# A decoder layer on one core: the transposed band masks of cross attention go from TensorE to GpSimd, in new instruction orders

## The chip, the cores and the metric

One core of one Trainium2 chip runs the whole program in one launch. The metric is the device time of one execution in microseconds (us); less is better.

## The reference, cut to what matters

32 samples (128 tokens x 128 features, float32) go through one decoder layer. After each block x is added and a layer norm without weights follows:

- **Self attention**, 16 heads of width 8, where queries, keys and values are all x itself: softmax(y y' / sqrt(8)) times x, per head, then one product with a 2048x128 matrix.
- **Cross attention**, 16 heads of width 8, queries from x, keys and values from a context of 128 tokens, with a band mask:

```python
mask = abs(i - j) <= 64                     # i: query, j: key, both 0..127
scores = where(mask, Q @ K.T / sqrt(8), -inf)
attn = softmax(scores); out = (attn @ V) @ Wo.T + bo
```

- **A local transformer of two layers** (8 heads of width 64, rotary position factors, a causal mask of 64 back, then a gated MLP), called local 0 and local 1.

## The kernel before, in words

A sample is the unit of work: all 128 tokens lie on the 128 partitions. There are four attention stages (self, cross, local 0, local 1) and two MLPs, and they work on different samples at the same time: while self attention has sample n, cross attention has n-1, local 0 has n-3 (its MLP's second part n-4), local 1 has n-4 (n-5). The dictionary `SKEW` (line 51) says this. A hardware loop of 26 passes is the main part; six iterations' worth of code ahead of it (`FILL`) fill this pipeline and a last part drains it.

Each engine has an instruction queue of its own and runs it strictly in order. What stands in it is written out by hand as strings of letters (`ORDER_TENSOR`, `ORDER_VECTOR`, `ORDER_SCALAR`, `ORDER_GPSIMD`, lines 74 to 97): one for the fill, one for the loop's pass, one for the drain. A letter stands for the next step of a stage: S self, Z self's values (x times the 2048x128 matrix), C cross, A and B the first parts of local 0 and 1, D and E their score parts, M and N the MLPs' first, O and P their second parts; W is a filler product. A stage is a Python generator, each `yield` ends a step, and `weave` (line 154) takes the steps in the string's order; a letter whose stage has no step left does nothing. Between engines only semaphores order the work (`wait_ge`, `then_inc`).

The attention core of self and cross (`core16`, line 626) on TensorE goes like this, by two pairs of head groups (a group is four heads and one PSUM bank of 512 columns):

- `head_scores` (593): natural scores, query on the partition, in bf16. For cross, `mask_band` (573) adds a mask of 0 or -1e30 by products of a mask tile with the identity: four products of 64x64 by 256 columns for a pair. VectorE takes the row maxima with negative sign (`head_max`, 1032).
- A transpose turns the negative maxima; ScalarE copies them back (`shifts`, 872).
- `turned_scores` (607): the transposed scores, key on the partition, in float32 (L611), then the maxima added by small products (L617), and for cross again `mask_band` (L579). ScalarE makes the exponentials into `s.e` in SBUF (`exps`, 877), four instructions of 128x512.
- Cross then sums with the tile `own` for the denominators (L717) and with V for the numerators (L724). Both wait for all exponentials. VectorE takes the reciprocal (L1108), multiplies (L1112), and TensorE projects (L729).

Each pair of cross has its own wait: the second pair's transposed scores wait for the first pair's exponentials, since they use the same two banks. The banks of self and cross are also lent to the MLPs of local 0 and 1.

GpSimd has no access to PSUM and does small SBUF work: products with the reciprocal denominators of the local layers (L1313), rotary additions (L1296, L1300), inverse roots by a power (L1245, L1292), copies and bias additions.

Of the kernel before, what the change touches and what calls it, by code (L numbers as in the profile page):

```python
# [34 lines left out]
GH = 4  # L35
# [39 lines left out]
    ("SZSZSZSSSZSSSSSSSSWWWWWWWWWWWSCCZSZCCSZCCSZCSCSCCSCSCCSSCSSCSCLSAASCAACSZZZSCCAZSASSCCDDCSSCCCSSCCCSSDCDSCDCSD"  # L75
     "MAAMAOOCAOCSBZBSCZBSCABSASSZZDCSSCDBBSCSCCCEECCCSSDDSCDCSDCEMEEMAOEONAAONSBPPBAPBZZSCBCSAZASZSSCCDDBBCSSCEECSS"
     "CCCDSSDCCDCSDSCEEMCECME"),
    ("ONAOAONABPSPBABPZSCZBSACAZSDSCSDCZSSCCBBSSCEECCCSDDSSDCCCSDEEMCCECME"),
    ("ONAOAONASPBPABSBPZZSCBACSZSSCCAZSCSCDDBCBSSCCEECSDCCCDSSCCDECSEDEMAEAMNOOAAONBPPBBPAACBCDCDCBBCCECECCCDCCCDCCD"
     "CEDEMAEAMEOOAAOBNBAABDDBWWWWWWWBNBDEEDPDDEMEPMEOOEPOBNBWWWNBPBPWWWWWWBBWWEEWWWWWWWWWWWWPEEWWEWWENWWWWWWWNPPWWP"))  # L80
ORDER_VECTOR = (
    ("SSSSSSSSSSSSSSSSSSSCCCSSCCSSCCLSSSSCSSSCSSCCSCLSSSSSAAAAACSCSCASSCCCCDDDSDSSDSDSSSCSCSSCSCSDMCMMSMSASAOAOCCCAA"
     "SSBBSSBBBCACCCDSDDSBSDODEESDSSSEESSECSCSESDCMMMSCMSCENNNONAOAAPABBABSPSSBBSSCCCABCCDDDPCCDEEDESOSDSSESSSEESSSD"
     "MSSCPMMCSMCCSECS"),
    ("NNNONOAAAAPABBPSSBPSSCCCABBDCDCBCDCSDSDESEDSESSESSPSESESSDSMSMMCCSMCOCEC"),
    ("NNNONOAAAAPASBBSPBSSBCCCBACCPCCDDDBSDDSESEDEESSSESOSCECSSSCCSDMCMMSMENSNNAAONAOPAAASOPBBPBBBCCCPBCCDDCCDDDEEED"
     "EECCPECCDCMMMMEAAAOAAOANBNBBBDNDBDBNDDDEEEEEDEMMMOMPOEOPNPNNNBBBBBBEEEEEPPEPENOPNNPNPPPP"))
# [6 lines left out]
ORDER_GPSIMD = (
    ("SSSSCSCSSASACAAAABDDCAMMSSASOAAABBBABBDDECEMMCNSNBASASAAABBBBABDODCEPEMMCS"),
    ("ONBSANASABAAPBABBBDDEECSMMC"),
    ("NSNOSBACAAAABBBBPABDDEECMMNNBSAAAAABBBBABCDDEPECMMNBOAAAAAABBNBBDBDEMEMNNBBBOOBBBPEENPNP"))
ORDER_SYNC = (
# [1268 lines left out]
```

## Time and profile before

| | |
|---|---|
| median of 3 runs | 1370.85 us (1366.49 to 1371.11) |
| the profiled execution | 1365.17 us, span 1363.4 us |
| TensorE busy | 1298.9 us, 95% |
| VectorE busy | 1069.0 us, 78% |
| ScalarE busy | 979.1 us, 72% |
| GpSimd busy | 761.7 us, 56% |
| one pass of the loop | 39.93 us |
| granted clock of TensorE | 0.991 of full |

Busy times count what an engine executes, not waits. The ends of matrix products are modelled, so two products that overlap show more time than they hold the queue: the distance between two starts is the price. Since the loop repeats exactly, an instruction seen at 602.02 us is also found at 641.95, one period later. "Released by" behind an idle time names what the engine waited for.

### The profile page before, as it was taken

How to read it: one execution, taken by the hardware profiler on the slowest of the kernel's cores; microseconds unless marked ns; L12 is line 12 of the kernel's file. 1: busy time of each engine (PE TensorE's matmuls, PEld its weight loads, DVE VectorE, ACT ScalarE, POOL GpSimd, SP SyncE). 2: the span in 40 equal slices, each digit the busy share in tenths (PEclk: the TensorE clock that was granted, in tenths of full speed). 3: DMA queues.
4: the chain of work that ended last, by engine and by line, in shares of the span. 5: the costliest groups of instructions: out<-in, count | busy, mean ns of one | idle time of the engine just before them, and what ended most of it. 6: DMA issues, size and time to landing. Idle time of an engine off the chain costs nothing. (4 is left out here: it accounts for less than half of the span.)

```text
span 1363.4 us, 41792 instructions
## 1 busy us (share of the span) xinstructions
PE 1298.9 (95%) x13550; PEld 906.1 (66%) x13550; DVE 1069.0 (78%) x3190; ACT 979.1 (72%) x2688; POOL 761.7 (56%) x843
## 2 busy tenths in 40 slices
PE   5999999999999999999999999999999999999876
PEld 2566666777766677766667777666777666776653
DVE  3667888888888888888888888888888888888743
ACT  2357777777787777778777777777777777777753
POOL 1135666555666555566655566565556666555653
PEclk9799999999999999999999999999999999999989
DMA  5000000000000000000000000000000000000000
GB/s 168 11 5 2 6 8 7 6 2 6 6 6 4 6 6 2 6 6 6 4 6 6 2 6 6 4 6 6 6 2 6 6 4 6 6 3 4 6 1 6
DMA packets 21042, 12.44 MB, mean 9 GB/s; under 512 B 4700, under 2 KB 19846, under 8 KB 20998
## 3 DMA queue, kind: packets, MB, share of 16 engines
q1 hardware_dynamic: 18790, 8.04, 2.2%
q10 hardware_dynamic: 2208, 3.84, 0.8%
q8 instruction: 24, 0.39, 0.1%
q14 instruction: 20, 0.16, 0.0%
HBM read 9.78 MB, written 2.10 MB: 9 GB/s over the span
## 5 line engine op out<-in xcount | busy, mean ns | idle before, releaser
L1292 POOL TENSOR_TENSOR local_rn<-local_sc,half_neg 128x8 f32<-128x8 f32 x128 | 211.0, 1649 | 69.3 <-DVE local_sc L1143 69.3
L1313 POOL TENSOR_TENSOR local_e<-local_e,local_rd 128x512 f32<-128x512 f32 x128 | 133.3, 1041 | 197.2 <-DVE local_rd L1160 197.2
L954 ACT ACTIVATE local_e<-local_ps,local_bias,local_rn 128x128 f32<-128x128 f32 x512 | 229.4, 468 | 13.2 <-DVE local_bias L1156 13.1
L668 PE MATMUL self_ps<-self_z,self_e 128*128 128x129 f32 x1024 | 146.0, 285 | 2.4 <-ACT self_e L881 1.1
L690 PE MATMUL local_ps<-wz,self_kT 128*128 128x512 f32 x256 | 138.2, 625 | 5.9 <-ACT self_kT L887 5.7
L1075 DVE SCALAR_TENSOR_TENSOR self_y<-self_ps,self_rd,self_y 128x128 f32<-128x128 f32 x448 | 133.1, 345 | 9.5
L668 PEld LDWEIGHTS self_ps<-self_z,self_e 128*128 128x128 f32 x1024 | 127.4, 192 | 11.6 <-DVE self_y L1075 2.3
L1296 POOL TENSOR_TENSOR local_cosp<-local_cosp,local_sinp 128x512 f32<-128x512 f32 x64 | 81.4, 1272 | 87.1 <-DVE local_sinp L1135 87.0
L1151 DVE TENSOR_REDUCE local_m<-local_ps 128x4 f32<-128x512 f32 x128 | 87.9, 687 | 39.0 <-PE local_ps L589 38.2
L934 ACT ACTIVATE local_sq<-local_ps 128x512 f32<-128x512 f32 x128 | 76.0, 594 | 48.4 <-PE local_ps L750 43.6
L954 ACT ACTIVATION_READ_ACCUMULATOR local_e<-local_ps,local_bias,local_rn 128x1 f32 x512 | 109.8, 215 | 0.0
L1036 DVE TENSOR_REDUCE self_neg<-self_ps 128x4 bf16<-128x512 f32 x128 | 82.6, 686 | 27.5 <-PE self_ps L598 26.7
L881 ACT ACTIVATE self_e<-self_ps 128x512 f32<-128x512 f32 x128 | 69.7, 596 | 34.7 <-PE self_ps L617 34.6
L1131 DVE TENSOR_TENSOR local_cosp<-local_ps,cos_t 128x512 f32<-128x512 f32 x128 | 87.8, 686 | 7.1 <-ACT local_sq L934 6.3
L1036 DVE TENSOR_REDUCE cross_neg<-cross_ps 128x4 bf16<-128x512 f32 x128 | 86.5, 683 | 6.9 <-PE cross_ps L579 6.6
L961 ACT ACTIVATE local_eT<-local_ps 128x512 f32<-128x512 f32 x128 | 70.6, 597 | 27.8 <-PE local_ps L789 27.7
L965 ACT ACTIVATE local_oT<-local_ps 128x512 f32<-128x512 f32 x64 | 39.5, 617 | 68.7 <-PE local_ps L797 68.7
L904 ACT ACTIVATE self_z<-local_ps 128x512 f32<-128x512 f32 x128 | 76.0, 599 | 16.6 <-PE local_ps L690 14.7
L1135 DVE TENSOR_TENSOR local_sinp<-local_ps,sin_t 128x512 f32<-128x512 f32 x128 | 87.0, 680 | 0.0
L1140 DVE TENSOR_REDUCE local_ss<-local_sq 128x8 f32<-128x512 f32 x128 | 86.3, 674 | 0.0
L1300 POOL TENSOR_TENSOR local_cosp<-local_cosp,local_sinp 128x512 f32<-128x512 f32 x64 | 81.1, 1267 | 1.5 <-DVE local_sinp L1135 1.4
L750 PE MATMUL local_ps<-wqkv_s,local_xT 128*128 128x512 f32 x128 | 70.3, 632 | 6.6 <-ACT local_xT L930 6.6
(179 smaller groups left out, 3322.8 us busy)
## 6 DMA issues: line engine op xcount, KB each, us to landing
self_xin<-x SPq DMA_DIRECT2D x32, 64.0 KB, 1.8
cross_cin<-ctx_in SPq DMA_DIRECT2D x32, 64.0 KB, 1.8
out<-local_out SPq DMA_DIRECT2D x32, 64.0 KB, 1.6
wqkv_s<-wqkv ACTq DMA_DIRECT2D x2, 768.0 KB, 9.7
wz<-w_heads ACTq DMA_DIRECT2D x4, 256.0 KB, 5.9
w_r<-w ACTq DMA_DIRECT2D x2, 341.0 KB, 11.0
con<-consts SPq DMA_DIRECT2D x1, 640.0 KB, 6.7
wo_s<-wo ACTq DMA_DIRECT2D x2, 256.0 KB, 10.8
```

The costliest lines, as they stand in the source:

```text
L668: last = nc.tensor.matmul(bank[:, 129 * j:129 * j + 129], s.e[:, h0 + j, :], s.z[:, h0 + j, :], start=True, stop=True)
L690: nc.tensor.matmul(LOC[l].b1 if g % 2 else LOC[l].b0, s.kT[:, :], wz[:, 512 * g:512 * g + 512], start=True, stop=True).then_inc(s.z_psum, 4)
L954: nc.scalar.activation(s.e[:, a, p, :], bank[:, 128 * p:128 * p + 128], ACT.Exp, bias=s.bias[:, a, p:p + 1], scale=s.rq[:, a, p:p + 1], ac ...
L1036: nc.vector.tensor_reduce(s.neg[:, 32 * g:32 * g + GH], (s.odd if g % 2 else s.even).rearrange("p (j t) -> p j t", j=GH), AX.X, ALU.max, n ...
L1075: nc.vector.scalar_tensor_tensor(out=s.y[:, h % 2, :], in0=bank[:, j, 0:128], scalar=s.rd[:, h:h + 1], in1=before, op0=ALU.mult, op1=ALU.a ...
L1131: nc.vector.tensor_tensor(s.cosp[:, a, :, :], heads, cos_t[l][:, a, :].unsqueeze(1).to_broadcast([128, LH, LD]), ALU.mult)\
L1135: nc.vector.tensor_tensor(s.sinp[:, a, :, :].rearrange("p h (u d) -> p h u d", u=2), halves[:, :, ::-1, :], sin_t[l][:, a, :].rearrange("p ...
L1140: nc.vector.tensor_reduce(s.ss[:, LH * a:LH * a + LH, 0:1], s.sq[:, a, :, :], AX.X, ALU.add)\
L1151: nc.vector.tensor_reduce(s.m[:, a, :], bank.rearrange("p (c t) -> p c t", c=LH // 2), AX.X, ALU.max, negate=True)\
L1292: nc.gpsimd.tensor_tensor(s.rn[:, heads], s.sc[:, heads], half_neg[:, 0:LH], ALU.pow).then_inc(done, STEP)
L1296: nc.gpsimd.tensor_tensor(s.cosp[:, 0, :, :], s.cosp[:, 0, :, :], s.sinp[:, 0, :, :], ALU.add).then_inc(s.k_roped, STEP)
L1313: nc.gpsimd.tensor_tensor(s.e[:, a, :, :], s.e[:, a, :, :], s.rd[:, a, :].unsqueeze(2).to_broadcast([128, LH // 2, 128]), ALU.mult)\
```

## The change

`mask_band` is no longer called for the transposed scores (it still is for the natural ones). The exponentials outside the band are therefore some finite number, and GpSimd sets them to zero in `s.e`: two `affine_select` instructions for each pair of head groups, each over 8 heads and one half of the query columns, 128x512 elements in all. Denominators and numerators wait for a new semaphore `band_done` in place of `exp_done`. Cross attention has two steps fewer on TensorE and two more on GpSimd. The order strings of all engines are new. In the loop's string of GpSimd most letters do nothing, since their stage has no step left.

```diff
...
 ORDER_TENSOR = (
...
-    ("ONAOAONABPSPBABPZSCZBSACAZSDSCSDCZSSCCBBSSCEECCCSDDSSDCCCSDEEMCCECME"),
+    ("ONAOAONABPSPBAPBSCBZSZCZSAASCSCDDZCSSCBBSSEECSDCCSDCCDSDSEEMCCECME"),
...
 ORDER_VECTOR = (
...
-    ("NNNONOAAAAPABBPSSBPSSCCCABBDCDCBCDCSDSDESEDSESSESSPSESESSDSMSMMCCSMCOCEC"),
+    ("NNNONOAAAPABBPSSAASSBCCCBBCCDDDBCCPDSSDSEESDSSEESESESOSDSSSMMSMCCMCCPECS"),
...
 ORDER_SCALAR = (
...
-    ("KOAANBAPSBASYBZCZBAASCZSSZDSSBBDCDDEEDDCCEEDCCEEEM"),
+    ("KOAANBPSABASBCBYZZCSAAZSSZDSSBBDDDCEECCDDEEDCCEEEM"),
...
 ORDER_GPSIMD = (
...
-    ("ONBSANASABAAPBABBBDDEECSMMC"),
+    ("NSNNNNNNBNNNAASOAAAAOBAAAAABOAAAAABBBBBBBOBBBBBAAAAAODAAABBBBBBDDEDAACBBCEBEBBDDDDCPPPPPEEBEBAAMEDEBMBDSSSSMSS"
+     "SSESESSSSMMMMAMMMACCCCCCCCCCCCCCCCC"),
...
 ORDER_SYNC = (
-    "CSP")
+    "SPC")
...
@@ -309,6 +310,7 @@
         CROSS.o_ready = sem("cross_o_ready")
         CROSS.proj_psum = sem("cross_proj_psum")
         CROSS.x_bias = sem("cross_x_bias")
+        CROSS.band_done = sem("cross_band_done")
         LOC[0].kept = sem("local0_kept")
         LOC[1].base_bias = sem("local1_base_bias")
         for s, n in ((SELF, "self"), (CROSS, "cross")):
@@ -615,13 +617,10 @@
                     for g in pair:
                         rows = slice(32 * g, 32 * g + 32)
                         last = nc.tensor.matmul(scores_bank(s, g)[:, 128 * j:128 * j + 128], hot_b[rows, j, :], s.negT[rows, :],
-                                                start=False, stop=(j == GH - 1 and not s.windowed), skip_group_check=True)
-                        if j == GH - 1 and not s.windowed:
+                                                start=False, stop=(j == GH - 1), skip_group_check=True)
+                        if j == GH - 1:
                             last.then_inc(s.scores_t_psum, 4)
                 yield
-                if s.windowed:
-                    mask_band(s, pair, s.scores_t_psum)
-                    yield
 
             def core16(s, v):
 
@@ -711,7 +710,7 @@
                 yield
                 yield from core16(s, v)
 
-                pe.wait_ge(s.exp_done, v + STEP)
+                pe.wait_ge(s.band_done, v + STEP)
                 for j in range(GH):
                     for g in range(G):
                         last = nc.tensor.matmul(s.b1[32 * g:32 * g + 32, 0:128], own[:, j, 32 * g:32 * g + 32],
@@ -1269,6 +1268,16 @@
                     pool.wait_ge(s.resid, v)
                 nc.gpsimd.tensor_tensor(s.xb[:, :], s.x[:, :], bo_r[:, :], ALU.add).then_inc(s.x_bias, STEP)
                 yield
+                for k, pair in enumerate(s.pairs):
+                    pool.wait_ge(s.exp_done, v + 8 * k + 8)
+                    heads = slice(GH * pair[0], GH * pair[0] + 2 * GH)
+                    late = s.e[:, heads, 64:128]
+                    nc.gpsimd.affine_select(late, late, [[0, 2 * GH], [-1, 64]], ALU.is_ge, 0.0, base=0, channel_multiplier=1)\
+                        .then_inc(s.band_done, 4)
+                    early = s.e[:, heads, 0:64]
+                    nc.gpsimd.affine_select(early, early, [[0, 2 * GH], [1, 64]], ALU.is_ge, 0.0, base=64, channel_multiplier=-1)\
+                        .then_inc(s.band_done, 4)
+                    yield
                 inverse_root(s, v, s.moments, s.ve, s.rs[:, :], s.rstd)
                 yield
```

In words, as far as the loop's pass is concerned, TensorE's steps from local 0's K product to cross attention's denominators are, before and after (`ts` transposed scores, `hs` natural scores, `m` the masks behind them, 0 and 1 the pair, `av` self attention's products with the values in sets of three heads):

```
before: ... self negT, D scores, self ts0, cross hs0, D mask, cross hs0 m, Z, self ts1, cross hs1, m, B qT, kT,
        self av0, av1, cross negT, E scores, E mask, cross ts0, m, self av2, D eT0, eT1, self av3, av4, D av,
        cross ts1, m, self av5, D projection, E eT0, eT1, M shift, cross denominators
after:  ... self negT, A qT, kT, self ts0, cross hs0, m, D scores, D mask, Z, cross hs1, self ts1, cross m, B qT, kT,
        self av0, av1, E scores, E mask, cross negT, self av2, D eT0, cross ts0, self av3, D eT1, cross ts1, D av,
        self av4, D projection, self av5, E eT0, eT1, M shift, cross denominators
```

ScalarE's from self attention's third group of exponentials on (`e` exponentials):

```
before: self e2, e3, B qT, kT, D e, cross negT, D e (two steps), E e (two), D eT0, eT1, cross e0, e1, E e (two), D oT, cross e2, e3
after:  self e2, e3, B qT, kT, D e (three steps), cross negT, E e (two), cross e0, e1, D eT0, eT1, E e (two), D oT, cross e2, e3
```

GpSimd's from local 0's weights on:

```
before: D weights 0, 1, E weights 0, 1, cross x + bias, S root, M bias, M root, C root
after:  D weights 0, 1, E weights 0, cross x + bias, selects of pair 0, E weights 1, selects of pair 1, P root, M bias, M root, S root, C root
```

## Rows read from the trace of the kernel before

**Rows 1.** The page, part 1: busy us (share of the span) and instructions, whole run.
```profile
PE 1298.9 (95%) x13550; PEld 906.1 (66%) x13550; DVE 1069.0 (78%) x3190; ACT 979.1 (72%) x2688; POOL 761.7 (56%) x843
```

**Rows 2.** Busy time by window, one period: length, then busy us (x instructions) per engine.
```profile
600.81:640.74 39.93, 39.33 (x425) 27.90 (x421) 33.20 (x99) 30.48 (x85) 23.70 (x27) 1.00 0.02 5
```

**Rows 3.** Busy time by window: ahead of the loop, the loop, behind it.
```profile
0.00:188.00 188.00, 164.72 (x1517) 104.71 (x1518) 123.58 (x374) 103.05 (x269) 74.61 (x93) 0.95 0.12 35
188.00:1227.00 1039.00, 1023.27 (x10955) 725.55 (x10954) 864.00 (x2578) 792.79 (x2185) 616.67 (x678) 1.00 0.02 5
1227.00:1364.00 137.00, 110.95 (x1080) 75.83 (x1078) 81.42 (x242) 83.23 (x236) 70.39 (x74) 0.97 0.02 4
```

**Rows 4.** Timeline of TensorE, 600 to 645 us: start us, duration us, instruction, count.
```profile
600.47 0.41 PE L589 MATMUL local_ps<-mask_n,ident_b 64*64 64x512 bf16 x4
...
607.75 0.30 PE L579 MATMUL cross_ps<-mask_w,ident_b 64*64 64x256 bf16 x4
607.99 0.49 PE L668 MATMUL self_ps<-self_z,self_e 128*128 128x129 f32 x2
...
610.34 1.08 PE L717 MATMUL cross_ps<-cross_e,con 128*32 128x128 f32 x32
...
617.48 1.10 PE L750 MATMUL local_ps<-wqkv_s,local_xT 128*128 128x512 f32 x2 [0.15 <-ACT local_xT L930]
...
636.31 0.40 PE L598 MATMUL cross_ps<-cross_kb,cross_qmb 32*128 32x128 bf16 x8
636.63 0.30 PE L579 MATMUL cross_ps<-mask_w,ident_b 64*64 64x256 bf16 x4
636.87 0.66 PE L763 MATMUL local_ps<-con,local_cosp 128*128 128x128 f32 x4
```

**Rows 5.** Timeline of ScalarE, 600 to 641 us.
```profile
601.37 0.22 ACT L954 ACTIVATION_READ_ACCUMULATOR local_e<-local_ps,local_bias,local_rn 128x1 f32 x1
602.02 0.46 ACT L954 ACTIVATE local_e<-local_ps,local_bias,local_rn 128x128 f32<-128x128 f32 x1 [0.44 <-DVE local_bias L1156]
...
607.46 0.64 ACT L965 ACTIVATE local_oT<-local_ps 128x512 f32<-128x512 f32 x1
608.15 1.08 ACT L881 ACTIVATE cross_e<-cross_ps 128x512 f32<-128x512 f32 x2
...
636.63 1.08 ACT L881 ACTIVATE self_e<-self_ps 128x512 f32<-128x512 f32 x2
```

**Rows 6.** Groups by line and form: busy us, mean ns, idle before.
```profile
L881 ACT ACTIVATE cross_e<-cross_ps 128x512 f32<-128x512 f32 x128 | 69.8, 603 | 1.7 <-PE cross_ps L579 0.4
...
L579 PE MATMUL cross_ps<-mask_w,ident_b 64*64 64x256 bf16 x512 | 38.2, 289 | 0.0
```

**Rows 7.** Timeline of VectorE, 600 to 641 us.
```profile
600.99 0.69 DVE L1151 TENSOR_REDUCE local_m<-local_ps 128x4 f32<-128x512 f32 x1 [0.82 <-PE local_ps L589]
...
601.77 0.16 DVE L1156 TENSOR_TENSOR local_bias<-local_m,local_rn 128x4 f32<-128x4 f32 x1
```

**Rows 8.** Groups by line and form, GpSimd: busy us, mean ns, idle before.
```profile
L1313 POOL TENSOR_TENSOR local_e<-local_e,local_rd 128x512 f32<-128x512 f32 x128 | 133.3, 1041 | 197.2 <-DVE local_rd L1160 197.2
L1296 POOL TENSOR_TENSOR local_cosp<-local_cosp,local_sinp 128x512 f32<-128x512 f32 x64 | 81.4, 1272 | 87.1 <-DVE local_sinp L1135 87.0
...
L1226 POOL TENSOR_SCALAR mask_n<-con 128x512 bf16<-128x512 f32 x2 | 1.2, 620 | 4.4 <-DMA bo_r<-bo 4.4
L1226 POOL TENSOR_SCALAR mask_w<-con 128x256 bf16<-128x256 f32 x2 | 0.8, 407 | 0.0
...
L1226 POOL TENSOR_SCALAR ident_b<-con 128x128 bf16<-128x128 f32 x1 | 0.3, 301 | 0.7 <-DMA con<-consts 0.7
```

**Rows 9.** Timeline of TensorE, the last sample's cross denominators.
```profile
1281.62 1.08 PE L717 MATMUL cross_ps<-cross_e,con 128*32 128x128 f32 x32 [0.64 <-ACT cross_e L881]
```

More of the change, by code:

```diff
@@ L88 @@
-ORDER_SCALAR = (
-    ("SSSZSSZZZSSSCSCSZZCSSCCZZSSCCAASACSAZCZSZAASSCZDSSCCDDDCCDDDKAMAAOCACSBSZBZBYSABSASZZSSBBCDDCCDDECCEDDEEDEEMEA"
-     "OANABPBASSZBCZBCAZSZASSBBDSDSCDDECCEDDEEDCCEEEM"),
-    ("KOAANBAPSBASYBZCZBAASCZSSZDSSBBDCDDEEDDCCEEDCCEEEM"),
-    ("KOAANSABPSABYBZZCBSCZASSASZSBCDBDDDCCEDECCEDEDEEEAKMAOAANBPBYBCAABCBBDDCDDCCDECCEDEEDEEAEMAKOAABBAABBDDDBDBNDD"
-     "EEDEEPEEMEOBBNBBBBPYEEEEKEEENP"))
+    ("SZSZSZSSSZSSSSSSSSCWWWWWWWWWWWSCZSCCZCCSZZCSCSCSCSCSSSCCSSCLSSAAASCACSZZSZCCSAAZCSCSDDCSSCCSSCCSSDSCSDCDCDMAAM"
+     "COOACOBSABZZSBCBSCAZASZSSCDCSSDCBBSCCEESCCSDSDSCCDCSDEMEEMAOEONAAOSBANBPPZBSBPZSCZACSAZSCSCDDBBSCSCEESCSCCDSCC"
+     "DSSDSCCDEEMCEME"),
@@ new lines @@
+    ("ONAOAONABPSPBAPBSCBZSZCZSAASCSCDDZCSSCBBSSEECSDCCSDCCDSDSEEMCCECME"),
+    ("ONOAOABSABBNAPPSZBZPSACAZCSZSSCCDDSSCBBCSEECSCCSSDCCSDSEDCCECDEMAEANMAOONAOPBPBBPAACBCDDCCBCCBCDCCEECCDDCCECDE"
+     "MAEAMEAOONOBABAABDDBWWWWWWWBBNEEDDDPDMEEPMEOOEPOBNBBWWWNBPPWWWWWWBWWWWWWWWWWWWPBWWEEEEWWEWWENWWWWWWWNPPWWP"))
+ORDER_VECTOR = (
+    ("SSSSSSSSSSSSSSSSSSSCCCSCCSCSCSLSSSSCCSSCSCSLCSSSSSSASAAAACSSCCSSCCCCADDSDSSDDSSSSDSSSCSSCSCCSDCMMMMSAAOCOCAACA"
+     "BBBOSSBBSSCCABCCDDSDSDDEESSDESSSESSCCSECSECSDMMMCMSENNSONAOANASAABBPBSBSPSBSCCCAOCCDBDDDCCSPDESEDSSSSESESSESSE"
+     "SSCDCMSMMCMPCSCE"),
+    ("NNNONOAAAPABBPSSAASSBCCCBBCCDDDBCCPDSSDSEESDSSEESESESOSDSSSMMSMCCMCCPECS"),
+    ("NNONONAAAABBASPBSBPSBSPCCCACCDDBDCCSDSEDSESESSDSEESESCCSCCSDSMCMMSEMNOSNNAANOAOAPAAPSBBPBBBCCCDDCCDDDCCBDPEEEE"
+     "ECCECCDMOCMMMEAAAOAAONANNOBBBBDDBBNDDDDEPEEEEDEMMMMPOENPONPNNBBBPBBBPEEPOEEPEEENPNNNPPPP"))
@@ L94 @@
+ORDER_SCALAR = (
+    ("SSSZZZSSZSSCSSCZZCSZCCSSZCCSSAASACSAZZCASZASSCZSSCCDDCCDDDDDKAMAOCCABSABSBZZBYASZAZSSSSBCBDDCCDDCCDEEDEEDEEMEA"
+     "OASBANABPSZBBZCZSACAZSSBBDSSDCDDCCDECCDEEEDEEEM"),
+    ("KOAANBPSABASBCBYZZCSAAZSSZDSSBBDDDCEECCDDEEDCCEEEM"),
+    ("KOABASANBSBAPZBZYCZCSAAZSSSBBSDDCDECCDEDCCDEEDEKEEAAMONABPABBACACYBDDBDBCDDCCCCDEEDEEKEEAEAMAOBABAABBDDBBDDDED"
+     "NEDEEPEEMEOBBNBBPYBBEEEEEEEKNP"))
 ORDER_GPSIMD = (
-    ("SSSSCSCSSASACAAAABDDCAMMSSASOAAABBBABBDDECEMMCNSNBASASAAABBBBABDODCEPEMMCS"),
@@ L96 @@
[L96 to L97 removed]
+    ("SSSSSCCCCSSSAOAAAABACCDCDCMSSMAASAAABBCBABBDCDCEEMCMNSSBNAOAASBABABBACBDDPCCEEMMSC"),
+    ("NSNNNNNNBNNNAASOAAAAOBAAAAABOAAAAABBBBBBBOBBBBBAAAAAODAAABBBBBBDDEDAACBBCEBEBBDDDDCPPPPPEEBEBAAMEDEBMBDSSSSMSS"
+     "SSESESSSSMMMMAMMMACCCCCCCCCCCCCCCCC"),
+    ("NSONBASAABAABCBBABDCDECECOPMMNBSNAAAAAACBBBBDBOODCCEECMMPNBAAAAANABBBBBDDEMEMNNBPBBBBBEEPNNP"))
 ORDER_SYNC = (
[L99 removed]
+    "SPC")
```

10 lines of the change are left out of this document (removed).

## The prediction

> **What bounds the kernel now.** I read the page's busy times first: TensorE is busy 95% of the span, ScalarE 72%, GpSimd 56% [rows 1]. Then one pass of the loop: a period lasts 39.93 us and repeats to the hundredth, with TensorE busy for 39.33 of it, ScalarE for 30.48 and GpSimd for 23.70 [rows 2]. The 26 passes make 1039 of the 1363 us; ahead of them lie 188 us and behind them 137 us, in which TensorE is less full (165 and 111 us busy) [rows 3]. So in the loop TensorE's own queue sets the time, and time taken off that queue comes back in full, unless another engine makes TensorE wait. The timelines of one period show how near that is. From the first K product of local layer 0 (617.48) to the end of self attention's last transposed scores (636.31) TensorE never waits: 18.83 us. From there to cross attention's denominators (610.34, one period on 650.27) it takes 13.96 us, also without a wait [rows 4]; but ScalarE ends the last cross exponentials at 608.15 + 1.08 = 609.23 [rows 5], only 1.11 us before the denominators start. From the denominators to the next 617.48 are 7.14 us, with short waits: a chain over reciprocal, output projection, norm and transpose. That stretch keeps its instructions and, on TensorE, its order. So the period is 18.83 + 13.96 + 7.14 = 39.93, and the change has to be placed in it.
>
> **Removed.** Per sample TensorE loses eight mask products on the transposed scores: two groups of four. A group holds the queue from 607.75 to 607.99, or 0.24 us [rows 4] (the products, 289 ns each, overlap [rows 6]). That is 0.48 us per sample, 12.5 us in 26 passes and 15.4 us in all 32 samples. This is the most that the change can give from that part, some 1.1%.
>
> **Moved, first stretch.** Cross attention's second pair of natural scores (636.31 to 636.63, 0.32 us [rows 4]) now goes before self attention's last transposed scores. The first stretch becomes 18.83 + 0.32 = 19.15 us, the second loses the same 0.32. Following the new lists of the other engines I find no new wait in the first stretch: what they have to deliver (rotated Q and K, copies to SBUF, maxima) is there some tenths before it is used.
>
> **Moved, second stretch.** TensorE's own work there is now 13.96 - 0.32 - 0.48 = 13.16 us. ScalarE does the same list of work in it, in another order. I count from the end of self attention's last transposed scores. Local layer 1's mask group, at 640.40 (600.47 one period on) or 4.09 before, comes at 4.09 - 0.32 = 3.77. From that group to the first of this layer's exponentials pass 602.02 - 600.47 = 1.55 us, by way of the maximum and the bias on VectorE [rows 4, 5, 7]; I take 1.5, as a reciprocal no longer stands between the two. So these exponentials start at 5.27. ScalarE could take them at 4.9 (its list from 636.63 to 601.59 + 39.93 = 641.52 lasts 4.9 at most, and now begins some 0.15 after the scores), so it waits as before. From these exponentials to the end of the last cross exponentials ScalarE is packed: 609.23 - 602.02 = 7.21 us [rows 5]. The same work in the new order ends at 5.27 + 7.21 = 12.48. Ahead of the last two exponentials stands the copy of local layer 0's attention output, ending at 12.48 - 1.08 = 11.40; only with it can TensorE go on to that layer's output projection. From there self attention's last product, projection, transposes and shift take what 607.99 to 610.34 shows, 2.35 us [rows 4] (before, the short product stood first and the copy was there in time; now it stands behind the projection). So TensorE comes to the denominators at 13.8, not at 13.16: of the 0.48 us saved and the earlier score pair, 0.64 is lost again to ScalarE's queue.
>
> **Added: the selects.** GpSimd gets four affine selects per sample, each over 8 heads x 64 columns, 128x512 f32 in place. Their throughput is no matter: GpSimd has 39.93 - 23.70 = 16.2 us free per period [rows 2], so four may cost 4 us each before it becomes the bound. Their latency counts: the first pair's selects lie behind other work, but the denominators wait for both selects of the last pair. The trace has no select, so I bound it. Nearest below is a one-input operation of the same size, 620 ns; the 301 and 407 ns of the same operation with 128 and 256 elements show that this is a fixed 0.2 us and 0.83 ns per element. Above stand two-input operations of 1041 and 1272 ns [rows 8]. A select reads one input but also has to form and compare an index; I take 0.75 us, near the one-input row, and keep 0.6 and 1.27 for the range. Nothing excludes more. The Trainium skill (GPSIMD Engine Reference, Performance pitfalls for Q7 kernels) says that compare-then-select bodies run at 2.03 cycles per element as written and 1.03 when unrolled twice; an estimate from that page's 1.2 GHz and the fixed 0.2 us would be 1.07 or 0.64 us, that is, either end of my bounds, and no row here tells which.
>
> The denominators can then start at 12.48 + 0.1 (a hand-over between engines, as 601.68 to 601.77 on [rows 7]) + 2 x 0.75 + 0.05 = 14.1, against 13.8 by TensorE's own queue. **Period:** 19.15 + 14.1 + 7.14 = 40.4 us, 0.46 more than now, and 12 us in 26 passes. With 0.6 us per select it is 40.1 (+0.15, 4 us in all), with 1.04 it is 41.0 (+1.05, 27 us), with 1.27 41.4 to 41.6 (+40 us). Behind the last pair's selects on GpSimd stand three inverse roots and a bias addition; the nearest needed one, for layer 0's second norm, is wanted only after the reciprocal of the denominators (0.96 us), by which time it is ready, so I cost that at nothing. If that cover were gone it would be some 0.5 us per pass. GpSimd's selects of the first pair take the place ahead of layer 1's second weights; with 0.75 they end before those can start, so again nothing; from 1 us up they push the last pair's by some 0.2.
>
> **Outside the loop** six samples lose 0.48 us each (2.9 us) where TensorE is full, and where it is not, the wait for the last exponentials (0.64 us before the last denominators, [rows 9]) grows by two selects and a hand-over, 1.65 us, in perhaps two or three samples. I set the two against each other: zero, within 4 us. No DMA is added or moved past anything that waits: SyncE's list has its three independent steps in another order, and they are prefetches by most of a period.
>
> **Sum.** The profiled execution took 1365.2 us for a span of 1363.4; with +12 it would be 1377. The median of the three runs is 1370.85, 5.7 above the profiled one; a forecast for the median lies between 1377 and 1383, and I say 1381.
>
> **The rivals.** (a) *No change* (27%): the selects cost about 0.6 us, and the period comes out within 0.25 us of 39.93: 1364 to 1377. Measurement of this kernel can tell about 0.5%, 7 us, from no change. For it: the one-input row. Against: the select's extra work. (b) *Faster* (28%): the removed 0.48 us counts in full, 26 x 0.48 + 2.9 = 15 us, so 1356, or half of that. The place is the copy of layer 0's attention output on ScalarE: if that stands ready when TensorE has finished its product (10.8 by TensorE's own starts, against the 11.4 of my chain), and a select stays under (13.16 - 12.0 - 0.15) / 2 = 0.5 us with ScalarE that much earlier, TensorE remains the only bound. Against it is the packed ScalarE stretch; for it is that my 0.64 is a difference of long sums, good to 0.3. (c) *Clearly dearer selects* (14%): 1.04 us and more, as two-input rows; 1371 + 27 = 1398 or more; the denominators become the longest wait in the loop. In its extreme GpSimd is the bound from 4 us per select. The Trainium skill (GPSIMD Engine Reference, Elementwise side-by-side cycle accounting) gives about 12 cycles per element for data-dependent branching; by that page an estimate is 5.1 us per select, and the change would be a disaster; I give that 2 of the 14. (d) That the change does not take the masks out can be left aside: the diff leaves the natural scores' masks alone and removes the call for the transposed ones.
>
> **How the numbers follow.** My forecast (selects of 0.68 to 0.95 us, +8 to +22 us) has 31%. With (c) slower by over 0.5% has 45%, within 0.5% 27%, faster 28%. The range has to reach into (b), to 1359, and up to the two-input price, 1401; about 8% lies below and 10% above. The forecast's own range is 1376 to 1393.
>
> **What would show it.** Of the changed kernel I expect: no mask products after the transposed scores (256 in place of 512); a select at 0.75 us; a period of 40.4; denominators that start 0.15 us after a select's end, with TensorE idle there for 0.3 us in every period, named as waiting for GpSimd; and a wait of TensorE before layer 0's output projection, named as ScalarE's copy. If the period is 39.5 with no such waits, the ScalarE chain is what I got wrong; if the wait is there but longer, it is the select's price.

## The result and the profile after

The changed kernel takes 1392.98 us (median of 4 runs, 1388.37 to 1394.04), the one before 1369.2 in the same session: a ratio of 1.0185, 95% interval 1.0162 to 1.0207, so slower, by 1.6 to 2.1%. The profiled execution took 1392.2 us for a span of 1390.3, 26.9 more than the 1363.4 of before. The forecast was 1381 with 1359 to 1401 as the range: the sign and the range held, the size did not. The median is 24 us above that of before, where the forecast's sum had +12 and its 1381 was 10 above the median it started from.

The page, part 1, of the changed kernel (against [rows 1]):

```profile
PE 1315.7 (95%) x13289; PEld 902.7 (65%) x13294; DVE 1072.7 (77%) x3190; ACT 976.1 (70%) x2688; POOL 841.7 (61%) x971
```

TensorE has 261 instructions fewer (of the 256 mask products and a few missing records) and is nevertheless busy for 17 us more: its products took longer somewhere. GpSimd has its 128 selects, 84 us by their groups (shown at the end).

Where the time went is read from one instruction per sample, the transpose of self attention's input. Timelines of TensorE, the seventh and the last of the 32, first after, then before:

```profile
230.30 0.27 PE L653 MATMUL self_ps<-con,self_x 128*128 128x128 f32 x1
...
1233.93 0.27 PE L653 MATMUL self_ps<-con,self_x 128*128 128x128 f32 x1
```

```profile
221.45 0.27 PE L654 MATMUL self_ps<-con,self_x 128*128 128x128 f32 x1
...
1218.95 0.27 PE L654 MATMUL self_ps<-con,self_x 128*128 128x128 f32 x1
```

The time up to the seventh (I call it the fill) is 8.85 us longer, the 25 periods between the two take 1003.6 in place of 997.5 (some 0.25 each), and from the last to the end, the drain, it is 1390.3 - 1233.93 = 156.4 in place of 1363.4 - 1218.95 = 144.45. So of 26.9 us the loop's passes have 6 to 7 and **the two ends have 20.8**. Some 4.7 of the 8.85 in the fill are no property of the kernel: they belong to a slow start that some executions of either kernel show (under e7).

The loop first. Busy time by window of the changed kernel, one period (against [rows 2]), then TensorE's and GpSimd's timelines around the denominators of that period (against [rows 4]):

```profile
588.77:628.97 40.20, 39.59 (x413) 27.48 (x414) 33.30 (x100) 30.37 (x84) 26.22 (x30) 1.00 0.02 5
```

```profile
607.83 0.30 PE L581 MATMUL cross_ps<-mask_w,ident_b 64*64 64x256 bf16 x4
...
611.52 0.41 PE L591 MATMUL local_ps<-mask_n,ident_b 64*64 64x512 bf16 x4
...
619.18 1.16 PE L802 MATMUL local_ps<-wo_s,local_oT 128*128 128x128 f32 x8
620.18 0.39 PE L667 MATMUL self_ps<-self_z,self_e 128*128 128x129 f32 x2
620.40 1.04 PE L788 MATMUL local_ps<-con,local_e 128*128 128x128 f32 x8
621.46 0.41 PE L816 MATMUL self_ps<-local_mid,con 128*128 128x64 f32 x2
621.80 1.08 PE L716 MATMUL cross_ps<-cross_e,con 128*32 128x128 f32 x32
...
628.97 0.67 PE L749 MATMUL local_ps<-wqkv_s,local_xT 128*128 128x512 f32 x1 [0.15 <-ACT local_xT L929]
```

```profile
620.24 0.66 POOL L1275 TENSOR_SCALAR_AFFINE_SELECT cross_e<-cross_e 128x512 f32<-128x512 f32 x1
620.85 0.66 POOL L1278 TENSOR_SCALAR_AFFINE_SELECT cross_e<-cross_e 128x512 f32<-128x512 f32 x1
```

The three stretches are 607.83 - 588.77 = 19.06, 621.80 - 607.83 = 13.97 and 628.97 - 621.80 = 7.17. The selects start 0.61 us apart and end at 621.51, 0.29 before the denominators, which follow the shift's product with no wait.

Now the ends. TensorE in the fill, after and then before:

```profile
32.88 0.46 PE L667 MATMUL self_ps<-self_z,self_e 128*128 128x129 f32 x2 [0.34 <-DVE self_y L1074]
36.83 0.45 PE L703 MATMUL cross_ps<-con,cross_cin 128*128 128x128 f32 x1 [3.48 <-DVE cross_x L1051]
...
37.71 3.29 PE L854 MATMUL local_ps<-hot_b,ident_b 128*128 128x512 bf16 x10 [0.22 <-issue]
40.83 0.27 PE L653 MATMUL self_ps<-con,self_x 128*128 128x128 f32 x1
```

```profile
28.77 2.54 PE L855 MATMUL local_ps<-hot_b,ident_b 128*128 128x512 bf16 x11
32.38 0.30 PE L654 MATMUL self_ps<-con,self_x 128*128 128x128 f32 x1 [1.08 <-issue]
32.62 0.30 PE L704 MATMUL cross_ps<-con,cross_cin 128*128 128x128 f32 x1
```

The fillers (products on a constant, which only keep TensorE busy) stood between attention and the next norm's result, where TensorE had nothing to do. The new order puts cross attention's transposes, which need that result, ahead of them: TensorE waits 3.48 us and then works off the fillers with everything ready. In the drain the changed TensorE waits for VectorE's row maxima and then runs slowly; the last sample's cross scores, after:

```profile
1287.50 0.40 PE L600 MATMUL cross_ps<-cross_kb,cross_qmb 32*128 32x128 bf16 x8 [0.60 <-DVE cross_qm L1100]
...
1290.26 0.39 PE L600 MATMUL cross_ps<-cross_kb,cross_qmb 32*128 32x128 bf16 x8 [1.55 <-DVE cross_neg L1035]
...
1292.60 0.26 PE L638 MATMUL cross_ps<-ident_b,cross_neg 128*128 128x128 bf16 x1 [1.13 <-DVE cross_neg L1035]
...
1293.65 2.08 PE L613 MATMUL cross_ps<-cross_qm,cross_kT 32*128 32x512 f32 x4
```

Before, the same four score products took 1.13 us behind shorter waits (0.68, 0.48 and 0.45 us). The windows name the cause: the granted clock (the third column from the end) is 0.62 and 0.70 after, and 1.00 from 1275 to 1295 in before, which holds the same work (counted from the last of the 32 transposes, both are 56 to 76 us). Busy time by window, after and then before:

```profile
1290.00:1300.00 10.00, 8.61 (x57) 5.11 (x59) 4.62 (x14) 5.55 (x19) 4.97 (x5) 0.62 0.01 2
1300.00:1310.00 10.00, 8.92 (x128) 6.89 (x124) 3.19 (x11) 7.80 (x24) 3.40 (x5) 0.70 0.00 0
...
1370.00:1380.00 10.00, 8.53 (x59) 5.54 (x60) 1.57 (x7) 3.29 (x6) 2.04 (x4) 0.62 0.01 3
```

```profile
1275.00:1285.00 10.00, 8.28 (x146) 5.67 (x147) 4.75 (x14) 9.59 (x36) 4.02 (x5) 1.00 0.01 2
```

The low stretch at 1370 has a wait in front of it as well. Twelve fillers stood behind the last score masks before; in the new order they run ahead of the scores, at 1359.03, and nothing is left to cover the softmax. TensorE before, then after:

```profile
1339.96 0.41 PE L589 MATMUL local_ps<-mask_n,ident_b 64*64 64x512 bf16 x4
1340.30 2.76 PE L855 MATMUL self_ps<-hot_b,ident_b 128*128 128x512 bf16 x12
```

```profile
1359.03 2.75 PE L854 MATMUL self_ps<-hot_b,ident_b 128*128 128x512 bf16 x12
...
1364.82 0.41 PE L591 MATMUL local_ps<-mask_n,ident_b 64*64 64x512 bf16 x4
1369.77 1.11 PE L788 MATMUL local_ps<-con,local_e 128*128 128x128 f32 x4 [4.53 <-POOL local_e L1322]
```

### The profile page after: what moved, and what is told of

Read it like the earlier page. It is cut to its first block and busy times, and to the rows that moved or that the text cites. A ratio compares the mean times of both kernels' runs of the same rounds, so it can differ in the third digit from the quotient of the medians.

```text
span 1390.3 us, 41520 instructions
## 1 busy us (share of the span) xinstructions
PE 1315.7 (95%) x13289; PEld 902.7 (65%) x13294; DVE 1072.7 (77%) x3190; ACT 976.1 (70%) x2688; POOL 841.7 (61%) x971
## 5 line engine op out<-in xcount | busy, mean ns | idle before, releaser
L667 PE MATMUL self_ps<-self_z,self_e 128*128 128x129 f32 x1024 | 151.7, 287 | 3.5 <-ACT self_e L880 2.5
L953 ACT ACTIVATION_READ_ACCUMULATOR local_e<-local_ps,local_bias,local_rn 128x1 f32 x512 | 120.8, 236 | 0.0
L903 ACT ACTIVATE self_z<-local_ps 128x512 f32<-128x512 f32 x128 | 73.1, 594 | 49.1 <-PE local_ps L689 49.1
L1244 POOL TENSOR_TENSOR local_rs<-local_ve,half_neg 128x1 f32<-128x1 f32 x96 | 55.8, 582 | 61.7 <-DVE local_ve L1180 54.7
L1035 DVE TENSOR_REDUCE cross_neg<-cross_ps 128x4 bf16<-128x512 f32 x128 | 82.3, 684 | 5.5 <-PE cross_ps L581 5.1
L788 PE MATMUL local_ps<-con,local_e 128*128 128x128 f32 x512 | 75.1, 279 | 7.4 <-POOL local_e L1322 7.3
```

The source lines that it names most:

```text
L667: last = nc.tensor.matmul(bank[:, 129 * j:129 * j + 129], s.e[:, h0 + j, :], s.z[:, h0 + j, :], start=True, stop=True)
L953: nc.scalar.activation(s.e[:, a, p, :], bank[:, 128 * p:128 * p + 128], ACT.Exp, bias=s.bias[:, a, p:p + 1], scale=s.rq[:, a, p:p + 1], ac ...
L1035: nc.vector.tensor_reduce(s.neg[:, 32 * g:32 * g + GH], (s.odd if g % 2 else s.even).rearrange("p (j t) -> p j t", j=GH), AX.X, ALU.max, n ...
```

## The experiments

An order is three strings per engine (ahead of the loop, the loop, behind it). The table has the ratio to the kernel before, and, of each profiled execution, the fill, the period and the drain as defined above; the sections below refer to it.

```
                     ratio (95%)               span    fill    period  drain
before               1                         1363.4  221.45  39.93   144.45
after                1.0185 (1.0162, 1.0207)   1390.3  230.30  40.20   156.37
e1_old_edges         1.0118 (1.0089, 1.0148)   1378.3  226.19  40.20   148.03
e2_old_orders        1.0108 (1.0079, 1.0137)   1377.2  225.50  40.08   150.66
e3_old_fill          1.0171 (1.0138, 1.0205)   1388.3  227.62  40.20   157.09
e4_old_drain         1.0111 (1.0081, 1.0142)   1386.5  231.29  40.20   151.11
e5_late_fillers      1.0167 (1.0139, 1.0194)   1386.6  225.74  40.20   157.24
e6_cross_fillers     1.0121 (1.0092, 1.0151)   1383.6  230.53  40.20   149.43
e7_fillers_first     1.0156 (1.0129, 1.0183)   1385.0  223.69  40.20   157.65
e8_no_masks          0.9988 (0.9969, 1.0007)   1365.3  225.40  39.86   144.21
e9_selects_aside     1.0184 (1.0162, 1.0206)   1385.4  225.47  40.20   156.26
e10_one_group_kept   1.0042 (1.0023, 1.006)    1367.7  222.87  39.99   145.80
e11_scores_earlier   1.0094 (1.0076, 1.0111)   1374.7  222.36  40.19   148.37
e12_both_edges       1.009  (1.0073, 1.0106)   1383.6  226.83  40.21   152.92
```

The fill of after, e4, e6, e8 and e12 contains the slow start, that of the others doesn't; only fills with the same start can be compared.

The first set splits the new orders from the selects.

**e1_old_edges.** The selects and the loop's new strings stay; the strings ahead of and behind the loop are those of before, adapted.

```diff
-TENSOR, VECTOR, SCALAR, GPSIMD = (new fill, new loop, new drain)
+TENSOR, VECTOR, SCALAR, GPSIMD = (old fill, new loop, old drain)
+# old: less TensorE's two steps C of masks, plus two steps C of selects on GpSimd
```

> The changed kernel's loop orders, but fill and drain in the orders of the kernel before (the steps of the transposed masks taken out, GpSimd's selects put in where the exponentials ended in the trace of before). Theory A (the orders of fill and drain cost 20 of the 27 us: fillers that moved onto the path in the fill, TensorE at the half clock in the drain): the period stays 40.20, the fill is within 3 us of before's, the drain within 4 us of before's, and the time is 7 to 13 us above before. Rival B (the selects' latency costs it where TensorE is not full, whatever the order): the edges stay 15 to 20 us longer than before's and the time is 22 to 27 us above before.

Measured: +1.18%, some 16 us, with 6.6 in the loop, 4.7 in the fill and 3.6 in the drain of the profiled execution. That is above the 7 to 13 us of theory A and below the 22 of rival B. The new orders at the ends cost about 0.7%, 9 us, by themselves. It doesn't come down to my loop term alone: with selects the ends stay some 8 us above before. The timeline of this kernel names most of that. At four of its denominators outside the loop TensorE waits for GpSimd's select, 6.0 us together (the fourth, at 173.68, is 0.99); before waited 0.64 at one of the four.

```profile
86.07 1.08 PE L707 MATMUL cross_ps<-cross_e,con 128*32 128x128 f32 x32 [1.91 <-POOL cross_e L1269]
...
1258.85 1.08 PE L707 MATMUL cross_ps<-cross_e,con 128*32 128x128 f32 x32 [1.56 <-POOL cross_e L1269]
...
1296.37 1.94 PE L707 MATMUL cross_ps<-cross_e,con 128*32 128x128 f32 x32 [1.57 <-POOL cross_e L1269]
```

**e2_old_orders.** The same with the loop's strings too.

```diff
-TENSOR loop "ONAOAONABPSPBAPBSCBZSZCZSAASCSCDDZCSSCBBSSEECSDCCSDCCDSDSEEMCCECME"
+TENSOR loop "ONAOAONABPSPBABPZSCZBSACAZSDSCSDCZSSCCBBSSCEECCSDDSSDCCSDEEMCCECME"
-GPSIMD loop (new)
+GPSIMD loop "ONBSANASABAAPBABBBDDCCEECSMMC"
```

> The whole change in masks and selects, but every part in the orders of before, with the same insertions. Theory A: the denominators now wait for the second select, 609.23 + 0.1 + 2 x 0.63 = 610.6 against 609.86 by TensorE's own queue, so the period is 39.93 - 0.48 + 0.74 = 40.2, the same as with the new orders, and the time is 7 to 13 us above before. Rival B: period 40.2 but 22 us or more above before. Rival C (the new orders hide the selects and the old ones do not): period 40.7 or more.

Timeline of TensorE, the denominators of one period:

```profile
615.76 1.08 PE L707 MATMUL cross_ps<-cross_e,con 128*32 128x128 f32 x32 [0.22 <-POOL cross_e L1269]
```

Here the wait for the selects does show, 0.22 us, and yet the period is 40.08, shorter than the 40.20 of the new order, which has no such wait. The reordering buys nothing in the loop. The period is 0.1 under the 40.2 of theory A, the time, 14 us above before, a little over its 13.

**e3_old_fill** and **e4_old_drain** take back one end each.

```diff
-(new fill, new loop, new drain)
+(old fill, new loop, new drain)     # e3
+(new fill, new loop, old drain)     # e4
```

> The changed kernel with only the fill in before's orders. Theory A: the loop and the drain stay as in the changed kernel (40.20; 154 us from the last self transpose to the end), the fill gets 3 to 8 us shorter: the time is 17 to 23 us above before. Rival B: no gain, 25 us above before.

> The changed kernel with only the drain in before's orders. Theory A: from the last self transpose to the end 142 to 147 us in place of 154, with at most two short stretches at the half clock in it: 13 to 18 us above before. Rival B: 154 us stays, 25 us above before. Rival D (the half clock in the drain is chance of the one execution profiled): the clock is full but the median time is no better than the changed kernel's.

The old drain gives 0.7%, 10 us of 24. The old fill gives 0.14%, inside both intervals: the expected 3 us and more didn't show. The profiles say why. e3's fill is 227.62, and with the same start the new fill takes 225.74 (e5) and 225.47 (e9): the old one has no misplaced fillers, but waits 1.91 and 1.00 us for selects, as in e1. So the 9 us of e1 are those of the drain. The drain of e4 is 151.1, 4 above the most I expected: the granted clock is low there too (0.69 from 1293 to 1303).

The second set changes single places of the ends.

**e5_late_fillers.** In the drain's tail the last scores of the local layers go ahead of the twelve fillers again.

```diff
-...WWWWWWBWWWWWWWWWWWWPBWWEEEEWWEWWENWWWWWWWNPPWWP
+...WWWWWWBBWWEEWWWWWWWWWWWWPEEWWEWWENWWWWWWWNPPWWP
```

> The changed kernel with one edit in TensorE's drain string: its last 47 letters in before's order, which puts twelve filler products behind local layer 1's last scores, where TensorE sits idle for 4.5 us, in place of ahead of them. Theory A (the drain is longer because TensorE falls to the half clock behind idle stretches): the 10.2 us at the half clock near the end shrink to 3.4 or less, and the time falls by 3 to 5 us against the changed kernel. Rival B (the drain is longer by the selects' latency, and the clock costs nothing on a chain of waits): within 1 us of the changed kernel.

A miss: -0.2% with overlapping intervals, and a drain as long as before the edit. In its profile the window from 1370 has a clock of 0.80 in place of 0.62, but from the last cross denominators to the end it takes 86.4 us, where the changed kernel takes 85.6 and before 81.8. So this place alone is not shown to be worth anything, and the 4 us of the tail are not explained.

**e6_cross_fillers.** e5, and 13 more fillers (2, 6 and 5) where TensorE waits for the row maxima of the last sample's cross scores.

```diff
-..."CDDCCBCCBCDCC"...
+..."CDDWWCCBWWWWWWCCBWWWWWCDCC"...
-wait_ge(LOC[0].resid, STEP * (B - 1 if n < EARLY_GAPS else B))
+wait_ge(LOC[0].resid, STEP * (B - 2 if n < 13 else B - 1 if n < 13 + EARLY_GAPS else B))
```

> As the run before, and thirteen more filler products, in the three waits of TensorE for row maxima among the last sample's cross scores (2, 6 and 5 of them; 0.21 us each at the full clock). Theory A: the 13.7 us at the half clock around the last cross scores go, and the time falls by another 5 to 7 us, to some 9 to 11 below the changed kernel. Rival B: no change, or 1 to 2 us more for the added products.

Confirmed: 0.64% less than the changed kernel, some 9 us (0.46% less than e5), by adding work to TensorE. Timeline of TensorE and a window of this kernel:

```profile
1291.53 1.24 PE L846 MATMUL self_ps<-hot_b,ident_b 128*128 128x512 bf16 x5
...
1293.47 1.13 PE L605 MATMUL cross_ps<-cross_qm,cross_kT 32*128 32x512 f32 x4
```

```profile
1293.00:1303.00 10.00, 8.50 (x154) 5.98 (x153) 4.21 (x12) 8.15 (x29) 6.20 (x7) 1.00 0.01 2
```

The score products start at 1293.47 against 1293.65, so the wait itself was worth 0.2 us. They take 1.13 against 2.08 us, and the last denominators come at 1300.16 in place of 1304.67: what the waits cost was the clock behind them, 4.3 of the 4.5 us up to there. The profiled executions agree. Counted from the last of the 32 transposes:

```
                                              to the last cross denominators   clock, 60 to 70 us
before; e8                                    62.7; 62.3                       1.00; 0.83
new drain (after, e3, e5, e7, e9)             70.7, 70.6, 70.9, 70.9, 70.7     0.50 in all five
new drain with the 13 fillers (e6, e12)       66.0, 66.8                       1.00, 0.83
old drain with the selects (e1, e2, e4)       66.1, 66.5, 66.5                 0.59, 0.54, 0.57
```

All five executions of the new drain without these fillers take 2.08 us for the score products, both with them 1.13: this fall of the clock is no chance. The 3.4 to 3.8 us that the old drain with selects stands above before are its waits for them (1.56 and 1.57 us in e1, against 0.64) and the slower products behind.

**e7_fillers_first.** One letter of the fill moved: cross attention's transposes behind the fillers.

```diff
-SZSZSZSSSZSSSSSSSSCWWWWWWWWWWWSC...
+SZSZSZSSSZSSSSSSSSWWWWWWWWWWWCSC...
```

> The changed kernel with one letter of TensorE's fill string moved: the first cross transposes stand behind the eleven filler products again, so that the fillers run while the first norm is computed. Theory A: the distance between the first two self transposes falls by 3 us (35.9 to 33 with the late rise of the clock, 28 to 29 without), and so does the time. Rival: later waits in the fill take it back, and the time stays within 1 us. The slow first products up to 28 us are the same instructions as in before, so I expect them to be chance: in some executions the clock rises at 15 to 18 us here too.

-0.3%, 4 us, but the intervals overlap, so the time alone doesn't show a gain; the profiles do. Self attention's second transpose comes at 33.14 in place of 40.83. Only about half of that is the order. The rest is a state of this execution, the slow start: in the profiles of the changed kernel, e4, e6, e8 and e12 the first score products of self attention take 2.08 us, in the other nine 1.13, with the same instructions up to there.

```profile
18.67 2.08 PE L613 MATMUL self_ps<-self_qm,self_kT 32*128 32x512 f32 x4 [0.43 <-ACT self_negT L874]
```

```profile
18.42 1.13 PE L604 MATMUL self_ps<-self_qm,self_kT 32*128 32x512 f32 x4 [0.43 <-ACT self_negT L865]
```

The twelfth run has the same slow start and e7's order, and from self attention's last products to its next transpose it takes 37.20 - 32.85 = 4.35 us where the changed kernel takes 40.83 - 32.88 = 7.95: the order's part is 3.6 us. With a fast start it is less: up to the seventh transpose e7 is 1.8 and 2.1 us ahead of e9 and e5, and with the slow start e12 is 3.5 ahead of the changed kernel. e9 and e5 have the changed kernel's fill and a fast start: against the 230.30 of the changed kernel that puts the slow start at 4.6 to 4.8 us, and what the fill itself costs above before at 4.0 to 4.3, not 8.85.

**e12_both_edges.** e6 and e7 in one kernel.

> The changed kernel with the three edits on TensorE's edge strings together (fillers ahead of the first cross transposes, fillers behind local layer 1's last scores, thirteen fillers in the last sample's cross waits). Theory A: the gains add, 3 to 4 us in the fill and 8 to 10 in the drain: 12 to 14 us above before, of which the loop has 7. Rival: a low clock comes back elsewhere in the drain, and it stays at 16 or more above before.

1.0090, and 1.0185 without the three edits: 13 us of 25 come back, as theory A has it, though the clock fell once more in this execution's drain (0.70 from 1360 to 1370).

The third set asks what the mask products and the selects are worth by themselves.

**e8_no_masks.** The kernel before without the masks on the transposed scores and with nothing in their place, its orders less those steps. Half of cross attention's mask is left out.

```diff
-                if s.windowed:
-                    mask_band(s, pair, s.scores_t_psum)
-                    yield
```

> The kernel before with the band masks on the transposed scores left out and nothing in their place: weights outside the band stay, so cross attention is computed without half of its mask. It measures the removal by itself, in before's orders. By the sum in the prediction the period falls by all of 0.48 us to 39.45 and the time by 12 to 15 us. Rival (ScalarE's chain is the bound there already): the period falls by 0.2 or less, the time by under 6 us.

This decides the question of the gain in the orders of before. TensorE has 0.48 us less to do per sample, and the period falls by 0.07. Even with no selects at all the removal brings 0.12% (-0.31% to +0.07%). TensorE's timeline of this kernel shows where the rest stays:

```profile
603.76 0.41 PE L581 MATMUL local_ps<-mask_n,ident_b 64*64 64x512 bf16 x4
...
611.42 1.16 PE L792 MATMUL local_ps<-wo_s,local_oT 128*128 128x128 f32 x8
612.42 1.04 PE L778 MATMUL local_ps<-con,local_e 128*128 128x128 f32 x8
613.29 0.33 PE L806 MATMUL self_ps<-local_mid,con 128*128 128x64 f32 x2
613.56 1.08 PE L706 MATMUL cross_ps<-cross_e,con 128*32 128x128 f32 x32
```

and ScalarE's:

```profile
605.31 0.46 ACT L943 ACTIVATE local_e<-local_ps,local_bias,local_rn 128x128 f32<-128x128 f32 x1 [0.44 <-DVE local_bias L1145]
...
610.71 0.66 ACT L954 ACTIVATE local_oT<-local_ps 128x512 f32<-128x512 f32 x1
```

From local layer 1's mask group to its first exponentials it is 605.31 - 603.76 = 1.55 us, as before; from there ScalarE's list reaches the copy of layer 0's output after 5.40, before 607.46 - 602.02 = 5.44 [rows 5]. The copy ends 611.37 - 603.76 = 7.61 us after the mask group here and 608.10 - 600.47 = 7.63 before, and 0.05 behind it the output projection starts. So the chain from the mask group over VectorE and ScalarE takes the same time with or without the two mask groups that TensorE does meanwhile: they lay beside it. From the copy's end to the denominators it is 2.19, and 2.24 before; with 7.61 for 7.63 that is all of the 0.07. In before the projection started only 0.21 behind the copy, so TensorE's queue could gain little there. TensorE, before:

```profile
608.31 1.06 PE L803 MATMUL local_ps<-wo_s,local_oT 128*128 128x128 f32 x8
```

**e9_selects_aside.** The changed kernel with its selects on a tile of zeros, and the denominators waiting for the exponentials alone. The same half of the mask is left out.

```diff
-                pe.wait_ge(s.band_done, v + STEP)
+                pe.wait_ge(s.exp_done, v + STEP)
-                    late = s.e[:, heads, 64:128]
+                    late = s.aside[:, heads, 64:128]
```

> The changed kernel in its own orders, with the same selects on a tile beside the exponentials (of zeros), so that GpSimd is as busy and the denominators wait for the exponentials alone; the weights outside the band stay in, so cross attention is computed without that half of its mask. Theory A (ScalarE's chain is what bounds the new loop, the selects stand a hair behind it): the period falls from 40.20 by 0.1 us at most, to 40.1, still above before's 39.93 with 0.48 us of TensorE work gone; the time falls by 2 to 6 us against the changed kernel, edges included. Rival B (the wait for the selects is the loop's cost): the period falls by the whole of it and of the masks, to 39.7 or less.

A period of 40.20 and a ratio of 1.0184 against 1.0185: in the new orders nothing waits for the selects, in the loop or at the ends (its drain is 156.26, the changed kernel's 156.37).

The last two try for a version that beats both, on the kernel before's orders.

**e10_one_group_kept.** GpSimd's selects for three of the four groups of heads (two of 128x512, two of 128x256), TensorE's mask for the last, whose exponentials end latest.

```diff
+kept = s.pairs[1][1] if s.windowed and pair == s.pairs[1] else None
-if s.windowed: mask_band(s, pair, s.scores_t_psum)
+if kept is not None: mask_band(s, (kept,), s.scores_t_psum)
```

> A version between the two, in before's orders: GpSimd selects on three groups, and TensorE keeps its mask (two of eight products) for the last group, whose exponentials end last, so that no select stands behind the last exponentials. The denominators should wait for nothing new. By ScalarE's chain (theory A) the period is that of the run without masks, 39.86 to 39.93, and the time equal to before within 3 us. Rival C (TensorE's removed work counts as soon as no select is waited for): period 39.57, 9 to 11 us below before.

**e11_scores_earlier.** e10 with local layer 1's scores one product of self attention earlier in the loop, so that the chain of e8 starts sooner.

```diff
-TENSOR loop ...BBSSCEECSC...
+TENSOR loop ...BBSECESCSC...
-SCALAR loop ...BBDCDDEEDDCCEE...
+SCALAR loop ...BBDDCDEECCDDEE...
```

> The run before, with two edits in the loop's strings: TensorE makes local layer 1's scores and mask ahead of self attention's second value product, and ScalarE takes the first cross exponentials ahead of local 0's copies. ScalarE's 0.44 us of waiting for the bias inside its packed stretch should go. Theory A: the chain gets shorter by about 0.4 us, TensorE's removed work shows for the first time, and the period falls to 39.5 to 39.8; the time is 3 to 10 us below before. Rival C (ScalarE is not the bound): the period stays where the run before has it, or rises by the wait that the new place gives TensorE (0.3).

e10 is at +0.42%, 4 us, period 39.99: no gain, and by its interval a small loss, just outside the 3 us of theory A. e11 is at +0.94%, period 40.19, a miss: the scores now wait for their own input, and VectorE's bias is still late. TensorE and ScalarE of this kernel:

```profile
602.06 1.16 PE L776 MATMUL local_ps<-local_kT,local_qT 64*128 64x128 f32 x16 [0.22 <-ACT local_kT L940]
```

```profile
605.08 0.46 ACT L949 ACTIVATE local_e<-local_ps,local_bias,local_rn 128x128 f32<-128x128 f32 x1 [0.36 <-DVE local_bias L1151]
```

No version beat the kernel before. In before's orders e8 bounds what the removal can give, 2 us; that another order would shorten the chain and give more is not excluded, e11 only failed to.

## Why the prediction was right in sign and wrong in size

**What failed: "Outside the loop ... I set the two against each other: zero, within 4 us."** It was 20.8 us of the profiled 26.9, and still about 16 with the 4.7 of the slow start taken off: 4 in the fill, 12 in the drain. I weighed there what six samples lose in masks and gain in waits for selects, and didn't go through the new strings of the fill and the drain, which I had gone through for the loop. Three things stand in them: fillers behind a product that waits instead of ahead of it (e7, e12: 2 to 3.6 us); the last cross scores waiting 0.60, 1.55 and 1.13 us for VectorE without fillers, with half the clock behind them (e6: some 9 us, together with e5's edit, which alone showed 0.2% at most); and the fillers of the tail ahead of the scores, for which no price was shown. e1 puts the new orders of both ends at 9 us, e3 and e4 lay that in the drain, and e12 mends 13. The wait that I did weigh, two selects and a hand-over before the last denominators, isn't in the changed kernel at all (e9). It is in the old orders, at four samples and not two or three, and is most of the 8 us that remain in e1. What the tail behind the last cross denominators takes longer, some 4 us, stays open.

**The loop.** The period came near in part by luck: the path was right up to the projection of local layer 0, but behind it two terms were off in opposite directions, and the selects did not decide. First stretch 19.15 forecast, 19.06 measured; third 7.14, 7.17. In the second the mask group came 3.69 us in (3.77 forecast), and the output projection 7.66 later, at 11.35 (11.40 forecast, by ScalarE's copy): the wait that I expected is among the waits of the changed kernel's weight loads as 13.0 us in 55 times, 0.7 at the longest.

```profile
PEld local_ps L802 <- ACT local_oT L964: 13.0, 55, 0.7
```

The denominators came at 13.97: 13.8 was forecast by TensorE's queue and 14.1 by the selects. One mis-sized term is the **select: 0.75 us taken, 0.66 measured** and 0.61 from start to start. The nearest row, the one-input operation of 620 ns [rows 8], should have been taken as it was; forming and comparing an index costs nothing that shows. The last select ended at 621.51 - 607.83 = 13.68. The other is the **2.35 us for self attention's last product, projection, transposes and shift: 2.62 measured** for the same instructions in their new order (why is taken up below). So TensorE's queue decided, and not the selects, as the sum had it. With my own chain and 0.61 for the select the denominators would have been forecast at 13.85 and the period at 40.14, a little too low (and my +0.15 for selects of 0.6 us should have read +0.19). The period was thus 40.20 in place of 40.4, and 26 passes 7 us in place of 12. Of the estimates that I worked out from the Trainium skill (GPSIMD Engine Reference, Performance pitfalls for Q7 kernels) the 0.64 us of an unrolled body agrees with this row, and 1.07 doesn't.

**The removal's price.** I wrote that 0.64 of the second stretch is lost again to ScalarE's queue and gave the full 15 us to the rival *faster* (28%). e8 gives 0.07 per pass: 2 us, not 15. The rows of before spoke against that rival, since the 5.44 and the 1.55 us of the chain [rows 4, 5] contain none of the removed products, and the copy ended only 0.21 ahead of the projection. On the other hand the new order doesn't start the chain sooner for free: against e8 the first stretch grows by 19.06 - 18.82 = 0.24, the mask group comes 0.41 sooner in the second, and 0.48 goes between projection and denominators (2.62 against 2.14), where self attention's last product now stands (0.22) and the transposes and the shift take 0.26 longer. The shift writes a bank of self attention's and waits for VectorE to have added up self attention's products (`SELF.acc`). VectorE ends the last of them at 621.31 and the shift starts at 621.46; before, 609.22 and 610.08. So that wait fits the 0.26, but no run tested it. VectorE, after:

```profile
620.96 0.35 DVE L1074 SCALAR_TENSOR_TENSOR self_y<-self_ps,self_rd,self_y 128x128 f32<-128x128 f32 x1
```

**The rivals.** *No change* rested on selects of 0.6 us. They were about that cheap, and the time still grew. *Clearly dearer selects* fell with 0.66 us and with e9. That the loop alone is +0.5% and the whole +1.85% was in none of them.

**What I said would show it.** No turned masks: yes. TensorE idle for 0.3 us at the denominators, waiting for GpSimd: no in the changed kernel, 0.22 in the old order (e2). A wait for ScalarE's copy: yes.

## What to carry to other kernels

Going through one period instruction by instruction gave the loop to 0.2 us, in part by luck; where fill and drain have orders of their own, go through those too, and look for what stands ahead of a product that waits and for where the fillers went. Work taken off the fullest engine counts only if the chains over the other engines are shorter than what is left: find the last wait of that engine, follow it back to where it came from, and see whether the removed instructions lie on that chain or beside it. A reordering that should pay for a new wait has to be measured without the new operation (here, beside it: e2 and e9) before it is credited with anything.

## What the runs showed that I had not expected

- TensorE's waits in the drain cost more afterwards than while they last: 3.28 us of waits on the way to the last cross scores were followed by windows at a granted clock of 0.62 and 0.70, that is, partly at 1.2 GHz, where the same four products take 2.08 in place of 1.13 us. With thirteen filler products in those waits (e6, which also has e5's edit) it stayed at 1.00 there, and the kernel was 9 us shorter. The fall came in all five profiled executions with these waits.
- Two profiles can be compared only from a common instruction on: by windows from the span's start the clock around the last cross scores seems to differ between the changed kernel, e5 and e7 (0.62, 0.50 and 0.50 from 1290 to 1300), while from 60 to 70 us behind the last transpose it is 0.50 in all three. Elsewhere chance remains: e6 and e12 have the same drain string, and behind the last cross denominators they take 83.4 and 86.1 us.
- At the start of some executions (after, e4, e6, e8, e12) self attention's products run at little more than half their pace until about 28 us, though the window from 18 to 28 us of the changed kernel records a granted clock of 1.00; in the other nine they don't. It moves self attention's first outputs by some 4 to 5 us. It comes with old and new orders alike, so it is not the change's, but how many of the timed runs had it isn't known.
- An affine select in place on 128x512 f32 takes GpSimd 657 to 662 ns, as long as a plain one-input operation of the size within 7%. Groups by line and form of the changed kernel:

```profile
L1275 POOL TENSOR_SCALAR_AFFINE_SELECT cross_e<-cross_e 128x512 f32<-128x512 f32 x64 | 42.3, 662 | 24.0 <-ACT cross_e L880 20.8
L1278 POOL TENSOR_SCALAR_AFFINE_SELECT cross_e<-cross_e 128x512 f32<-128x512 f32 x64 | 42.1, 657 | 0.0
```
